# Adding the causal mask on VectorE, in the instruction that finds a diagonal chunk's peak, instead of on TensorE

## What is computed

```python
q_values = jnp.einsum('bir,bjr->bij', state, action) / SCALE        # first attention, one "head"
q_values = jnp.where(causal, q_values, -jnp.inf)
weights = jax.nn.softmax(q_values, axis=-1)
...
scores = jnp.einsum('bthd,bshd->bhts', q, k) * scale                 # second attention, 16 heads
causal = jnp.tril(jnp.ones((T, T), bool))
scores = jnp.where(causal[None, None], scores, -jnp.inf)
attn = jax.nn.softmax(scores, axis=-1)
y = jnp.einsum('bhts,bshd->bthd', attn, v).reshape(B, T, H * Dh)
```

## Time and profile before

| | |
|---|---|
| time, median of 3 executions | 2184.12 us (2183.26 to 2187.24) |
| the profiled execution's own time | 2182.38 us |
| its span, first to last instruction | 2180.6 us |
| mean granted TensorE clock | 0.992 of full speed |
| the first attention's tiles / the second attention | about 190 to 290 us / about 621 to 2045 us of the span |

### The profile page before, as it was taken

The page is one execution under the profiler, slowest core; times in us unless marked ns, Lnnn a source line. Parts: engine busy times, 40 slices in busy tenths (PEclk is TensorE's granted clock), DMA queues, the critical chain, the costliest instruction groups (busy, mean ns, idle before and its releaser), DMA issues. The chain is left out here.

```text
span 2180.6 us, 41705 instructions
## 1 busy us (share of the span) xinstructions
PE 2068.1 (95%) x14574; PEld 1820.4 (83%) x14574; DVE 1473.0 (68%) x3379; ACT 1339.3 (61%) x3382; POOL 908.1 (42%) x834
## 2 busy tenths in 40 slices
PE   5888978989989999999999999999999999999889
PEld 3665866657869999999999999999999998999778
DVE  6645757645367768777687777777777767777552
ACT  4223642224267777777787777777778768777552
POOL 0342002433243554545445355364454545535232
PEclk9999989999999999999999999999999999999999
DMA  5453042550000000000000000000000000000100
GB/s 203 101 115 54 2 147 58 141 118 1 32 13 6 4 9 11 4 6 9 8 6 9 6 4 13 6 4 6 9 9 6 9 6 9 4 2 1 45 10 30
DMA packets 50990, 67.32 MB, mean 31 GB/s; under 512 B 10080, under 2 KB 36960, under 8 KB 50656
## 3 DMA queue, kind: packets, MB, share of 16 engines
q1 hardware_dynamic: 40416, 51.80, 7.6%
q0 software_dynamic: 10368, 12.85, 3.5%
HBM read 49.15 MB, written 15.48 MB: 30 GB/s over the span
## 5 line engine op out<-in xcount | busy, mean ns | idle before, releaser
L988 ACT ACTIVATE phase_p<-phase_scores,phase_bias 128x512 f32<-128x512 f32 (+3 forms) x680 | 416.3, 626 | 86.4 <-DVE phase_bias L976 86.4
L1033 DVE TENSOR_TENSOR phase_pt_lo<-phase_ring,phase_pt_hi 128x512 fp32r<-128x512 f32 (+3 forms) x680 | 392.7, 605 | 102.7 <-ACT phase_pt_hi L1028 96.7
L969 DVE TENSOR_REDUCE phase_peaks<-phase_scores 128x1 f32<-128x512 f32 (+3 forms) x680 | 398.1, 602 | 59.6 <-PE phase_scores L958 51.9
L1028 ACT ACTIVATE phase_pt_hi<-phase_ring 128x512 fp32r<-128x512 f32 (+3 forms) x680 | 345.2, 534 | 132.8 <-PE phase_ring L1013 128.0
L122 PE MATMUL phase_y<-phase_pt_hi,phase_v_hi 128*128 128x256 f32 (+1 forms) x1152 | 343.2, 298 | 1.6 <-DVE phase_y_lo L1877 1.6
L1013 PE MATMUL phase_ring<-sb_ident,phase_p 128*128 128x128 f32 x2312 | 339.2, 273 | 4.5 <-ACT phase_p L988 2.8
L124 PE MATMUL phase_y<-phase_pt_hi,phase_v_lo 128*128 128x256 f32 (+1 forms) x1152 | 321.5, 279 | 0.0
L123 PE MATMUL phase_y<-phase_pt_lo,phase_v_hi 128*128 128x256 f32 (+1 forms) x1152 | 321.3, 279 | 0.0
L1013 PEld LDWEIGHTS phase_ring<-sb_ident,phase_p 128*128 128x128 f32 x2312 | 261.5, 140 | 26.6 <-ACT phase_p L988 7.3
L1892 POOL TENSOR_TENSOR phase_straight<-phase_rot,phase_rope 64x512 f32<-64x512 f32 x128 | 163.8, 1280 | 279.1 <-ACT phase_rot L1781 279.1
L1909 POOL TENSOR_TENSOR sb_x<-sb_x,phase_part 128x512 f32<-128x512 f32 x128 | 164.8, 1287 | 259.0 <-ACT phase_part L1816 256.5
(11 more groups left out here) (249 smaller groups left out, 4966.5 us busy)
## 6 DMA issues: line engine op xcount, KB each, us to landing
phase_e_up<-expert_up SPq DMA_DIRECT2D x32, 352.0 KB
phase_e_dn<-expert_down SPq DMA_DIRECT2D x32, 256.0 KB
y_rows<-phase_zero SPq DMA_DIRECT2D x8, 512.0 KB, 9.0
xn_rows<-phase_ln_xn SPq DMA_DIRECT2D x8, 512.0 KB, 6.4
sb_x<-y_rows POOLq DMA_DIRECT2D x8, 512.0 KB, 10.8
phase_raw_qk<-qk SPq DMA_DIRECT2D x16, 256.0 KB, 2.5
phase_raw_up<-up SPq DMA_DIRECT2D x10, 256.0 KB, 4.3
sb_x<-x SPq DMA_DIRECT2D x4, 512.0 KB, 7.0
```

The source lines that it names most:

```text
L969: dve.tensor_reduce(self.peaks[:, t % 2, c:c + 1], self.scores[:, at:at + self.width(t, c)], AX.X, ALU.max).then_inc(*self.peaked.one)
L988: act.activation(self.p[:, at:at + width], self.scores[:, at:at + width], ACT.Exp, bias=self.bias[:, t % 2:t % 2 + 1], accum_out=self.sums ...
L1028: act.activation(hi, value, ACT.Copy).then_inc(*self.t_hi.one)
L1033: dve.tensor_tensor(lo, value, as_f32(hi), ALU.subtract).then_inc(*self.t_lo.one)
```

## The change

The product with the mask goes. A tile `hide` of 128x512 bf16 takes the place of `mask_b`: its last 128 columns hold the old mask, loaded by the same DMA, and the 384 before them are set to zero by GpSimd at the start. For a diagonal chunk of width `w` VectorE adds the last `w` columns of `hide` to the scores, writes the sum back to the same PSUM bank, and keeps the row's maximum as the peak. Other chunks keep the old instruction. The order of the steps is the same.

```diff
-        self.mask_b = sb("mask_b", [P, P], BF16)
+        self.hide = sb("hide", [P, CH], BF16)
...
-        for out, name in ((core.ident, "ident"), (core.ident_b, "ident_b"), (core.mask_b, "mask_b")):
+        for out, name in ((core.ident, "ident"), (core.ident_b, "ident_b"), (core.hide[:, CH - P:], "mask_b")):
...
     def pool(self, pool):
         tag, core = self.tag, self.core
+        if self.start:
+            pool.memset(core.hide[:, 0:CH - P], 0.0)
         pool.memset(self.zero[:], 0.0).then_inc(*self.cleared.one)
...
     def pe_score(self, pe, key, pairs):
         h, t, c = key
-        diag, at = c == t // 4, self.bank(key) * BANK
-        n = max(256, self.width(t, c))
+        at, n = self.bank(key) * BANK, max(256, self.width(t, c))
         if old := self.old_chunk[key]:
             pe.wait_ge(*self.p_done[old])
         for k, (a, b) in enumerate(pairs(n)):
             done = pe.matmul(self.scores[:, at:at + n], a, b, start=k == 0, stop=k == len(pairs(n)) - 1)
-        if diag:
-            at += t % 4 * P
-            done = pe.matmul(self.scores[:, at:at + P], self.core.ident_b[:], self.core.mask_b[:], start=False, stop=True,
-                             skip_group_check=True)
         done.then_inc(*self.scored.one)
...
-        dve.tensor_reduce(self.peaks[:, t % 2, c:c + 1], self.scores[:, at:at + self.width(t, c)], AX.X, ALU.max).then_inc(*self.peaked.one)
+        w = self.width(t, c)
+        scores, peak = self.scores[:, at:at + w], self.peaks[:, t % 2, c:c + 1]
+        if c == t // 4:
+            dve.tensor_tensor_reduce(scores, scores, self.core.hide[:, CH - w:], 1.0, NEG, ALU.add, ALU.max, peak).then_inc(*self.peaked.one)
+        else:
+            dve.tensor_reduce(peak, scores, AX.X, ALU.max).then_inc(*self.peaked.one)
```

## The result

| | before | after |
|---|---|---|
| median of 9 runs each, same chip, us | 2187.24 (2183.26 to 2189.45) | 2173.84 (2171.99 to 2180.92) |
| ratio, 95% interval | | 0.9945 (0.9934 to 0.9957) |
| profiled execution, own time, us | 2182.38 | 2172.35 |
| its span, us | 2180.6 | 2170.6 |
| second attention, first to last bias on VectorE, us | 1418.6 (622.14 to 2040.78) | 1407.5 (622.40 to 2029.91) |

The changed kernel is 0.55% faster: 0.0055 x 2184 = 12 us, or 10.3 us under the median that stood before the prediction, where 21 were forecast; the two medians of nine are 13.4 us apart. The direction was right and the time lies in the range on record, but the gain is about half of what the sum promised. The stretches say where it came from: 11.1 us from the second attention, nothing from the first.

What follows compares the result with a forecast made beforehand. TensorE's queue was taken to bound the second attention. Removed slots worth 24.6 us less 3.5 given back made 21.1 us: 2163 us in the median's terms, 1.0% faster, range 2155 to 2177.

Steps and rivals of the forecast that it cites:

- The bound: Second attention: TensorE's own queue binds, with 8 us of waits in 1390, so a removed slot comes back as time.
- the term 16 x 0.08 = 1.3 us: First attention's 16 masks, priced at the smaller price, 0.08 us each, to be gained on TensorE.
- The product's price: TensorE, diagonal chunks: a mask costs 0.08 us before transpositions, 0.12 before another product; 24.6 us in all.
- The fused instruction: VectorE, diagonal chunks: main part at the plain peak's time, second instruction 0.09 us; VectorE's share about 76%.
- The rival of half pace: VectorE: fused instruction takes a second pass, 0.33 us more a tile; gain only 10 us, 2174; chance 0.13.
- the case quoted beside it: Trainium skill, VectorE: scalar-tensor-tensor with two SBUF sources that aren't bf16 runs at half throughput; no run shows it.
- The rival with VectorE as the bound: Diagonal chunk in VectorE's queue: fused instruction's extra time makes it the bound; 23 us slower, 2207; chance 0.10.
- The swallowed gain: ScalarE's and VectorE's queues pace the tiles, the short slot becomes a wait; within 0.2%, at 2183; chance 0.08.
- The range: Whole kernel's time: 2155 to 2177 us, the upper end taking in the half pace and its spread.
- the text's own bounds of slots and loss: Whole kernel: 32.6 us of slots without loss gives 2152, 16.3 less 5 gives 2173.
- Who waits for it: At 27 visible waits, 0.09 us of gain lost and 0.04 of delay added each: 3.5 us given back.
- the slack of one tile, 1.26 us: Second attention, one tile: from the end of chunk 0's exp to its transposition's start, covering the bias's 0.09 us delay.

Runs made afterwards that it cites:

- e3: Kernel before with the mask product issued twice in a row; 2198.27 us, ratio 1.0059.
- e2: Kernel before, product kept, diagonal chunk's peak found by the fused instruction adding a tile of zeros; 2185.81 us, ratio 1.0007.
- e1: Kernel before with the mask product left out and nothing in its place; 2171.67 us, ratio 0.994.
- e5: Changed kernel with tile 0's transposition in odd heads moved behind the next product with values; 2169.12 us, ratio 0.9936 against the kernel before.
- e6: Kernel before with tile 0's transposition in odd heads moved behind the next product with values; 2184.99 us, ratio 1.0001.
- e7: Changed kernel with plan letters moved in strings 0, 2, 4 and 6, one each; 2172.97 us, ratio 0.9952 against the kernel before.
- e10: Changed kernel with letters moved in strings 0 and 2, and in string 3 a product for y sent ahead; 2176.56 us, ratio 0.9962 against the kernel before.
- e9: Changed kernel with letters moved in strings 0 and 2 only; 2170.72 us, ratio 0.9937 against the kernel before.

## Why the prediction was right and wrong

**The bound**: right for the second attention. TensorE stays full and the gain comes out of its queue; e3 shows the same from the other side. For the first attention it was wrong: the term 16 x 0.08 = 1.3 us brought nothing, and e3's second product cost only 0.2 us there.

**The product's price**: right, 0.08 and 0.12 us, at every diagonal chunk where nothing else is late. By the slot figure of the Trainium skill ("TensorE: Matmul & The Clock Gate", Back-to-back issue gap: 134 cycles, 56 ns) the sum is an estimate of 15.2 us, which is closer to the 12 measured, but for another reason: e3's second product has that price, 0.06 us, and the removed one does not.

**The fused instruction**: right in its main part (690 and 292 ns where 685 and 285 were taken) and a little dear in its read (0.07 for 0.09). VectorE is at 76%. The rival of half pace fell with these rows. That no run shows the case quoted beside it is not quite so: in the kernel before L1235, a scalar-tensor-tensor form without a maximum, has both sources in SBUF and none in bf16, and takes 674 ns for 512 columns and 409 to 415 for 256, about 1.0 ns a column, no half pace. With a maximum kept, the case occurs in no run. The rival with VectorE as the bound fell too, since e2 costs under 3 us and not 23.

**The swallowed gain** was given 0.08 as an outright loss of everything. Something of that kind took half.

**The range** held in part by luck. Its upper end, 2177, was set for the half pace, which did not occur; the text's own bounds of slots and loss ended at 2173.

**The step that failed** is "Who waits for it", the term 27 x 0.13 = 3.5 us given back. In the second attention, 23.3 us of slots less the 11.1 that came are 12.2. Of these some 9 belong to the removal alone (23.3 - 14.1, e1) and some 3 to the fused instruction (e2). The term had 1.1 us (27 x 0.04) for the latter and 2.4 for the former. With the first attention's 1.3 us the account closes: 24.6 - 12.2 - 1.3 = 11.1.

What the term took wrongly is that the places with a visible wait, and only they, swallow a slot. Of the 27, the eight behind the chunk of tile 6 in odd heads wait 0.46 us each for the exp before and after (3.7 us together in both), and the full price came back there. Eight waits for k_lo, behind tile 5 in odd heads, stayed at 2.3 to 2.4 us together. Of the three groups of eight only that for the rest of y, also behind tile 5 in odd heads, grew, from 1.6 to 3.3 us. On the other side, the list of waits names where TensorE is late, and says nothing about where it arrives 0.14 us after its data. The text weighed the slack of one tile, 1.26 us.

The plan's strings repeat every two heads, so the traces can be matched place by place, from the last score product of one diagonal chunk to that of the next. With the change TensorE gains its 0.06 to 0.14 us nearly everywhere. It loses it behind the chunks of tiles 3, 4, 5 and 15 in even heads and of tiles 1, 5 and 15 in odd heads, where the distance changes by -0.01 to +0.27 us (medians over the heads). Against the prices these seven places fall short by 11.6 us in all, nearly the whole of the 12.2. Matched in the same way, e1 falls short by 8.2 us at the same seven places, of its 9.2, and e2 is longer by 2.6 us there, of its 2.7. So both losses sit at the same few places. The largest, tile 1 of odd heads, is +0.27 where -0.08 to -0.12 was due, 2.5 to 2.9 us in 8 heads, and it is the one that e5 gave back (2.8).

Why the data does not come earlier there is in the rows above: the exp's chain doesn't start at the mask. At tile 0 VectorE's peak stands behind the subtraction for the rest of y (714.03 + 0.41), not behind TensorE, so a mask less behind the score product makes the exp no earlier. From the last score product's start to the exp's end it went from 1.94 us (713.38 to 715.32) to 2.10 (712.81 to 714.91), and to 2.02 in e1, while TensorE's own way there became two masks shorter. That such a chain holds at the other six places too is only argued.

What stays open: one place is tested by an experiment of its own (e5, e6); at the others, where TensorE now waits for the rest of y, for k_lo and for v_lo, it is shown that the gain is lost there, and not why, since moves of letters there brought other waits in their place (e7, e10). Why the first attention returned nothing was not looked into.

The fastest kernel tried is e5, 2169.1 us and 0.64% under before. Its interval overlaps that of the change alone; its stretch is 2.8 us shorter.

## What to carry to other kernels

Price a slot taken from a full queue by what lies between starts, then go through the places behind it and write down the slack of each, the data's end against the user's start: a place with less slack than the slots removed ahead of it can give back the rest, and no list of waits shows it. A place with a wait need not lose anything: ask whether the awaited data comes earlier too when TensorE does. Doing one half of a change alone (the product gone, the new instruction added) separates the two losses at once. Before mending a weight loader's wait, look whether TensorE was streaming meanwhile.

## What the runs showed of the hardware

The sum-and-maximum in one VectorE instruction, from PSUM and bf16 SBUF back to PSUM, runs at the plain peak's pace (690 ns for 512 columns and 292 for 128, where the peak has 683 and 281). Its accumulator is read by an instruction of 138 ns, which delays the next one by 0.07 us only.

A single bf16 product of 128 columns between longer products costs more than a second one behind it: 0.08 us before a transposition, 0.12 before a product of 256 columns, 0.06 for the second in a row (e3).

A weight loader's wait of 0.23 us under a streaming matmul cost nothing: taken away in e9, the time stayed.

The mean granted clock of the first attention differed between executions, 0.99 to 1.00 in seven traces and 0.96 in five, and its stretch with it: 86.9 to 87.1 us against 88.3 to 89.5.

A scalar-tensor-tensor instruction of VectorE with two sources in SBUF, none in bf16, and no maximum kept ran at 1.0 ns a column (674 ns for 512 columns, before, L1235).
